# Scan stage of a two-layer network on one core: the sum over the states as turned tiles, turned back ahead of the gate

## The chip, the core and the metric

The kernel runs on one core of a Trainium2 chip. The core has TensorE (matrix products into PSUM), VectorE, ScalarE and GpSimd, each with a queue of its own, and a queue (SyncE) that issues the transfers here. The engines wait for each other by semaphores. The metric is the time of one execution on the device in microseconds (us); less is better.

## What is computed

Two layers on x of shape (2, 2048, 128). Layer 0 is a Mamba block that runs forwards and backwards over the sequence, then a mixture of experts; layer 1 is retention and another mixture of experts. The change touches the Mamba block alone:

```python
u, z = split(x @ in_w.T, 2)                 # 256 channels each
u = silu(causal_conv4(u) + conv_b)
dbc = u @ xproj_w.T                         # rank 64, B: 16 states, C: 16 states
dt = softplus(dbc[..., :64] @ dt_w.T + dt_b)
def step(h, inp):                           # for each channel d and each state n
    h = exp(dt * A) * h + dt * u * B
    return h, einsum('bdn,bn->bd', h, C)    # the sum over the 16 states
y = ys + u * D
return y * silu(z) @ out_w.T                # the gate, and the output projection
out = x + mamba(x, forwards) + mamba(reversed x, backwards)
```

## The kernel before

All of it is float32, apart from the parts of B and C that are spread over the partitions. The Mamba stage works in 16 units (`UNITS`): 8 chunks of 512 positions, each once forwards (even units) and once backwards (odd units). The 256 channels are two halves (`HF`) of 128 partitions; a tile "128x1024" is both halves of a chunk. In a unit there are 16 steps, one for each state n; `s` counts all 256 steps. The five engines run lists of their own, written out by hand; each list goes through the steps s in order and has in it, at given n, the work for the chunk after next or the next (`prep(m + 1, n)`).

For a state s the work goes like this:

- ScalarE makes the decays exp(dt * A), one half at a time, into one of four PSUM banks `pa` (`decays`, line 588). These banks are slots: `handed()` (line 269) writes out in which order things are put into them, item i goes to `pa[i % 4]`, and item i may be written once item i - 4 has been taken (`s_taken`, counted by VectorE). Per unit the squares and the relu of the next chunk's dt pass through the same slots.
- The inflow dt*u*B is made by VectorE (`inflow`, line 731, with B spread by TensorE in `spread_b`) for nine of the states, by GpSimd (line 876) for the seven in `BY_G` = 1, 3, 5, 7, 9, 13, 15.
- VectorE scans (`scan`, line 742): one instruction for each half, in place in one of six buffers `hh`.
- GpSimd multiplies with C into one of four buffers `hc` (`times_c`, line 888); before writing the buffer of state s it waits until TensorE has added state s - 4.
- TensorE adds up (`add_up`, line 409): with the identity as weights and `hc` as the 512 moving columns, into the two PSUM banks `py`. TensorE does it four steps late (`LAG` = 4). The first product of a unit is the D term: `uz` times the diagonals `dd`. It waits for the gate of the unit before (`s_gate`), since `py` is one pair of banks.

After scan 3 of the next unit (`n == LAG - 1`) VectorE does the gate (line 757): `yz` = silu(z) times `py`, one instruction of 128x1024. TensorE's output projection (`out_project`) of that unit comes at n = 8 and 9 of the next unit but one in its own list (`prep(m + 1, n)`), that is in the unit after the gate's; ScalarE collects it (`collect`, line 583). In the list of ScalarE, n = 3 has the copies of rank and high part (`rank_and_high`), n = 5 the middle part (`mid_part`, line 506); VectorE takes the rest of high at n = 4 and the low part at n = 5 (`low_part`, line 699), and TensorE waits for the low part before dt is projected (n = 6).

At the end of the last unit nothing follows in this stage: the last sum, gate, projection and collection come one after the other, and then all engines meet (`phase_end`).

GpSimd's list has per unit 16 products with C, 7 inflows and, at n = 12, dt times u of the next chunk (line 867), for which VectorE's first inflow of the next unit waits.

## Time and profile before

| | before |
|---|---|
| time, median of 3 runs | 1487.87 us (1487.68 to 1488.51) |
| the profiled execution: span from first to last instruction | 1526.0 us |
| TensorE busy, matrix products | 1319.7 us, 86% |
| VectorE busy | 1240.1 us, 81% |
| GpSimd busy | 1154.2 us, 76% |
| ScalarE busy | 968.7 us, 63% |
| mean granted clock of TensorE, share of 2.4 GHz | 0.964 |

The profile is of one execution, which takes longer than the runs that are timed. The Mamba stage is its first part, up to about 933 us. In the rows PE is TensorE's products, PEld its weight loads, DVE VectorE, ACT ScalarE, POOL GpSimd; L423 is line 423 of the kernel. A row of instructions has output<-inputs, shapes, xcount. An f32 product shows as two records. The two levels of TensorE's clock are 1.00 (2.4 GHz) and 0.50 (1.2 GHz). Who ended a wait is inferred; where the engine named had long been done it was another.

### The profile page before, as it was taken

Reading aid. Unit: us, or ns where it says so; the run is one execution under the profiler, and the core shown is the slowest. Engines: PE = TensorE matmul, PEld = TensorE weight load, DVE = VectorE, ACT = ScalarE, POOL = GpSimd, SP = SyncE. Lnnn points to the kernel's source line nnn. Section 1 sums busy time; section 2 is a strip of 40 time slices with the busy share of each in tenths; the row PEclk is TensorE's granted clock in tenths of the full one; section 3 lists DMA queues with packets and bytes.
Section 4 is the critical chain, followed back from the end, with each engine's and each line's share of the span. In section 5 each row is a group of like instructions: output and inputs, shape, how many; then the busy total and the mean of one; then the engine's idle time right before and its main releaser. Section 6 shows DMA issues by size and latency. Waiting matters only on the chain.

```text
span 1526.0 us, 19904 instructions
## 1 busy us (share of the span) xinstructions
PE 1319.7 (86%) x6159; PEld 760.5 (50%) x6159; DVE 1240.1 (81%) x1990; ACT 968.7 (63%) x1810; POOL 1154.2 (76%) x683
## 2 busy tenths in 40 slices
PE   6799889889988988988988878988998999997595
PEld 2234334334434433433433334558996666666594
DVE  6999999999999999999999996323335888876376
ACT  6887878878778777787787774214554555542144
POOL 2899999999999999999999992611333555583542
PEclk9999999999999999999999989999999999999698
DMA  5323322333343333342333224131216000011223
GB/s 194 116 86 123 133 106 104 133 119 111 122 129 113 123 105 114 122 127 93 122 133 107 99 104 188 52 82 41 80 52 220 2 1 2 2 55 32 79 68 96
DMA packets 62888, 148.38 MB, mean 97 GB/s; under 512 B 9216, under 2 KB 34304, under 8 KB 53072
## 3 DMA queue, kind: packets, MB, share of 16 engines
q1 hardware_dynamic: 58016, 137.30, 26.6%
q0 software_dynamic: 4768, 9.81, 2.0%
q8 instruction: 51, 0.84, 0.2%
q14 instruction: 53, 0.43, 0.1%
HBM read 134.14 MB, written 18.56 MB: 100 GB/s over the span
## 4 chain that ended last, share of the span: by engine, by line
PE 32%; DVE 25%; issue 15%; POOL 12%; ACT 10%; another core or an unknown queue 3%; DMA 2%; SPq 1%; DVEq 0%; POOLq 0%; ACTq 0%
DVE hh L754 15%; POOL hc L895 8%; DVE hh L739 3%; PE py L423 3%; ACT pa L598 3%; PE pr L1806 3%; PE bank L1352 2%; PE bank L1348 2%; PE bank L1362 2%; POOL dtu L874 2%; PE pr L1820 2%; PE pr L2009 2%; ACT uz L492 1%; PE bank L1268 1%
## 5 line engine op out<-in xcount | busy, mean ns | idle before, releaser
L895 POOL TENSOR_TENSOR hc<-hh,cs 128x1024 f32<-128x1024 f32 x256 | 599.3, 2369 | 3.9 <-ACT st L603 2.6
L423 PE MATMUL py<-hc,ident 128*128 128x512 f32 x1024 | 487.5, 605 | 0.1
L754 DVE TENSOR_TENSOR_SCAN hh<-pa,st,hh 128x512 f32<-128x512 f32 x384 | 466.4, 1265 | 0.5 <-ACT pa L598 0.2
L598 ACT ACTIVATE pa<-dt,w 128x512 f32<-128x512 f32 x512 | 343.8, 684 | 184.4 <-DVE hh L754 183.2
L423 PEld LDWEIGHTS py<-hc,ident 128*128 128x128 f32 x1024 | 198.3, 195 | 220.5 <-issue 211.8
L885 POOL TENSOR_TENSOR hh<-dtu,bs 128x1024 f32<-128x1024 f32 x111 | 262.4, 2365 | 2.4 <-DMA bs<-bcrows 2.4
L739 DVE TENSOR_TENSOR hh<-dtu,pb 128x1024 f32<-128x1024 f32 x145 | 174.3, 1202 | 15.1 <-POOL dtu L874 14.1
L754 DVE TENSOR_TENSOR_SCAN hh<-pa,hh 128x512 f32<-128x512 f32 x128 | 147.8, 1205 | 2.0 <-ACT pa L598 1.0
L1478 POOL DMA_INDIRECT ytoken<-ysort,token x39 | 39.6, 1016 | 112.2 <-ACT ysort L1410 111.6
L335 PE MATMUL pq<-xn,w 128*128 128x512 f32 x248 | 118.0, 600 | 4.0 <-ACT xn L613 2.8
L1851 DVE TENSOR_SCALAR rot<-pr,b 128x128 f32<-128x128 f32 x184 | 51.8, 344 | 50.0 <-PE pr L1820 21.8
L406 PE MATMUL pb<-bc,sel 96*128 96x512 bf16 x145 | 56.4, 389 | 41.6 <-DVE hh L739 41.1
L1455 DVE TENSOR_TENSOR ht<-bank,xt 128x512 f32<-128x512 f32 x39 | 27.0, 692 | 69.3 <-PE bank L1362 66.0
L1806 PE MATMUL pr<-rot 128*128 128x128 f32 x368 | 53.9, 294 | 31.5 <-ACT rot L1833 22.2
L1869 POOL DMA_INDIRECT ytoken<-rot,token x46 | 44.8, 974 | 46.4 <-DVE rot L1858 38.4
L335 PEld LDWEIGHTS pq<-xn,w 128*128 128x128 f32 x248 | 47.4, 192 | 63.6 <-issue 61.7
L419 PE MATMUL py<-uz,dd 128*128 128x512 f32 x64 | 41.7, 787 | 38.0 <-DVE yz L762 36.3
L2486 POOL TENSOR_TENSOR qr<-ra,rb 128x256 f32<-128x256 f32 x16 | 11.6, 726 | 75.8 <-DVE rb L2252 75.8
L1806 PEld LDWEIGHTS pr<-rot 128*128 128x128 f32 x368 | 48.5, 206 | 34.7 <-ACT rot L1839 18.0
L1197 POOL DMA_INDIRECT xsorted<-xn,pos x32 | 30.9, 965 | 43.2 <-DVE pos L1170 29.2
L1290 ACT ACTIVATE xt<-bank 128x512 f32<-128x512 f32 (+1 forms) x32 | 18.1, 570 | 69.5 <-PE bank L1259 54.9
L406 PEld LDWEIGHTS pb<-bc,sel 96*128 96x128 bf16 x145 | 14.1, 97 | 95.4 <-DVE hh L739 65.3
(333 smaller groups left out, 2523.6 us busy)
## 6 DMA issues: line engine op xcount, KB each, us to landing
cs<-bcrows SPq DMA_DIRECT2D x64, 1024.0 KB, 4.6
bs<-bcrows SPq DMA_DIRECT2D x112, 256.0 KB, 4.4
xsorted<-in_pads SPq DMA_DIRECT2D x13, 387.0 KB, 5.3
rot<-in_rot SPq DMA_DIRECT2D x4, 1024.0 KB, 5.0
wx<-in_l_w SPq DMA_DIRECT2D x4, 1024.0 KB, 10.0
ysort<-ytoken SPq DMA_DIRECT2D x14, 256.0 KB
wx<-in_l_w SPq DMA_DIRECT2D x1, 3072.0 KB, 11.2
wx<-in_l_w SPq DMA_DIRECT2D x1, 2304.0 KB, 16.2
```

Source lines behind the costliest of these rows:

```text
L335: i = pe.matmul(bnk[:, :], w[:, W_U + t * DI + h * P:W_U + t * DI + (h + 1) * P], tokens(m, t), start=t == 0, stop=t == TAPS - 1)
L406: pe.matmul(pb[:, :], sel[0:96, s % NS:s % NS + 1].broadcast_to([96, P]), bc[s // NS % 2][0:96, :], start=True, stop=True).then_inc(s_b, 1)
L419: pe.matmul(py[:, h * CH:(h + 1) * CH], dd[s // NS % 2][:, h, :], uz[s // NS % 2][:, h, :], start=True, stop=False)
L423: i = pe.matmul(py[:, h * CH:(h + 1) * CH], ident[:, :], hc[s % HCS][:, h, :], start=False, stop=n == NS - 1)
L598: act.activation(pa[i % SLOTS][:, :], dt[m % 2][:, h, :], ACT.Exp, scale=wd[m % 2][:, W_A + h * NS + n:W_A + h * NS + n + 1]).then_inc(s_s ...
L739: v.tensor_tensor(hh[s % HHS][:, :, :], dtu[m % 2][:, :, :], pb[:, :].unsqueeze(1).broadcast_to([P, HF, CH]), ALU.mult).then_inc(s_db, 1)
L754: v.tensor_tensor_scan(hh[s % HHS][:, h, :], pa[i % SLOTS][:, :], hh[s % HHS][:, h, :], 0.0 if first else st[:, m % 2, n, h:h + 1], ALU.mu ...
L885: g.tensor_tensor(hh[s % HHS][:, :, :], dtu[m % 2][:, :, :], bs[i // BG][:, i % BG, :].unsqueeze(1).broadcast_to([P, HF, CH]), ALU.mult).t ...
L895: g.tensor_tensor(hc[s % HCS][:, :, :], hh[s % HHS][:, :, :], cs[j % 2][:, s % CG, :].unsqueeze(1).broadcast_to([P, HF, CH]), ALU.mult).th ...
L1806: i = pe.matmul(pu[j % 2][:, f * P:(f + 1) * P], wr[j % 2][:, f * P:(f + 1) * P], xts[j % 2][:, :], start=True, stop=True)
L1851: i = v.tensor_scalar(ht[j % 2][:, f * P:(f + 1) * P], pu[j % 2][:, f * P:(f + 1) * P], b1[:, ds(e * FK + f, 1)], 0.0, ALU.add, ALU.max)
L1869: g.indirect_dma_start(out=ytoken, out_offset=bass.IndirectOffsetOnAxis(ap=token[:, j:j + 1], axis=0), in_=ysort[:, j, :], in_offset=None) ...
```

## The change

In the sum over the states data and identity change sides. Each 128x128 piece of `hc` is now the stationary operand, the identity moves (128 columns), and the product is done as a transpose (`is_transpose=True`) that adds to what is in PSUM. So `py` holds the sum with positions on the partitions: eight pieces for each state. The D term is made in the same turned form (pieces of `uz` stationary, diagonals moving). When a unit is complete, ScalarE copies both banks of `py` into a new SBUF tile `yt` (`keep_sum`, at n = 4 of the next unit, behind the decays of state 5). TensorE turns the eight pieces back (`turn_back`, at n = 4 in its list) into two of the four decay slots, which `handed()` now lists behind the decays of state 5. The gate reads these two slots, as two instructions of 128x512, and has moved from behind scan 3 to behind scan 5. The D term of the next unit waits for the copy, not for the gate; the output projection waits for the second slot to be taken. Since TensorE fills some slots, the waits for ScalarE's fillings count with `slot_count`. Not shown in the diff: the new semaphores, and one semaphore (`s_wset`) in the place of two for the start's exponentials and diagonals, with its counts.

```diff
@@ -235,6 +236,7 @@
                 yz = sb(k, "yz", [P, HF, CH])
+                yt = sb(k, "yt", [P, HF * CH])
                 hh = [sb(k, f"hh{i}", [P, HF, CH]) for i in range(HHS)]
...
@@ -271,13 +273,20 @@
                         order += [("decay", s, h) for h in range(HF)]
+                        if m >= 1 and n == LAG + 1:
+                            order += [("y", m - 1, h) for h in range(HF)]
                         if m + 1 < UNITS and n in (10, 11):
                             order += [("square", m + 1, n - 10, h) for h in range(HF)]
                         if m + 1 < UNITS and n == 12:
                             order += [("relu", m + 1, h) for h in range(HF)]
-                    return order
+                    return order + [("y", UNITS - 1, h) for h in range(HF)]

                 turn = {item: i for i, item in enumerate(handed())}
+                by_tensor = [item[0] == "y" for item in handed()]
+
+                def slot_count(i):
+
+                    return i + 1 - sum(by_tensor[:i + 1])

...
@@ -365,7 +374,7 @@
                         if of[0] == 0:
-                            pe.wait_ge(s_gate, m + 1)
+                            pe.wait_ge(s_taken, turn["y", m, HF - 1] + 1)
                             if m + 2 < UNITS:
...
@@ -408,20 +417,31 @@
                         n = s % NS
+                        tiles = [(h, kt, slice(kt * P, (kt + 1) * P)) for h in range(HF) for kt in range(4)]
                         if n == 0:
                             if s >= NS:
-                                pe.wait_ge(s_gate, s // NS)
+                                pe.wait_ge(s_yt, s // NS)
                             else:
                                 pe.wait_ge(s_xt, 6)
                             if s // NS < 2:
-                                pe.wait_ge(s_diag, (HF + 1, 2 * HF + 1)[s // NS])
-                            for h in range(HF):
-                                pe.matmul(py[:, h * CH:(h + 1) * CH], dd[s // NS % 2][:, h, :], uz[s // NS % 2][:, h, :],
-                                          start=True, stop=False)
+                                pe.wait_ge(s_wset, (HF + 2, 2 * HF + 3)[s // NS])
+                            for h, kt, t in tiles:
+                                pe.matmul(py[:, h * CH + kt * P:h * CH + (kt + 1) * P], uz[s // NS % 2][:, h, t], dd[s // NS % 2][:, h, :],
+                                          start=kt == 0, stop=False)
                         pe.wait_ge(s_hc, s + 1)
+                        for h, kt, t in tiles:
+                            i = pe.matmul(py[:, h * CH + kt * P:h * CH + (kt + 1) * P], hc[s % HCS][:, h, t], ident[:, :],
+                                          is_transpose=True, start=False, stop=n == NS - 1 and kt == 3)
+                        i.then_inc(s_ysum, 1)
+
+                    def turn_back(m):
+                        pe.wait_ge(s_yt, m + 1)
                         for h in range(HF):
-                            i = pe.matmul(py[:, h * CH:(h + 1) * CH], ident[:, :], hc[s % HCS][:, h, :], start=False, stop=n == NS - 1)
-                        i.then_inc(s_ysum, 1)
+                            i = turn["y", m, h]
+                            pe.wait_ge(s_taken, i - SLOTS + 1)
+                            for kt in range(4):
+                                mm = pe.transpose(pa[i % SLOTS][:, kt * P:(kt + 1) * P], yt[:, h * CH + kt * P:h * CH + (kt + 1) * P], ident[:, :])
+                            mm.then_inc(s_yback, 1)

...
@@ -466,9 +486,12 @@
                             add_up(s - LAG)
+                        if n == LAG and m >= 1:
+                            turn_back(m - 1)
                         prep(m + 1, n)
                     for s in range(STEPS - LAG, STEPS):
                         add_up(s)
+                    turn_back(UNITS - 1)
                     out_project(UNITS - 1, (0, 1))
...
@@ -598,6 +621,13 @@

+                    def keep_sum(m):
+
+                        act.wait_ge(s_ysum, NS * (m + 1))
+                        if m >= 1:
+                            act.wait_ge(s_yback, HF * m)
+                        act.activation(yt[:, :], py[:, :], ACT.Identity).then_inc(s_yt, 1)
+
                     def keep_state(s):
...
@@ -670,6 +700,8 @@
                             diagonals(1)
+                        if s % NS == LAG and s >= NS:
+                            keep_sum(s // NS - 1)
                         prep(s // NS + 1, s % NS)
...
@@ -688,6 +720,7 @@
                     scalar_normed(xn, range(NT - 4, NT))
+                    keep_sum(UNITS - 1)
                     collect(UNITS - 1)
...
@@ -704,7 +737,7 @@
                             i = turn["square", m, f, h]
-                            v.wait_ge(s_slot, i + 1)
+                            v.wait_ge(s_slot, slot_count(i))
                             if f > 0:
...
@@ -750,17 +783,18 @@
                             i = turn["decay", s, h]
-                            v.wait_ge(s_slot, i + 1)
+                            v.wait_ge(s_slot, slot_count(i))
                             v.tensor_tensor_scan(hh[s % HHS][:, h, :], pa[i % SLOTS][:, :], hh[s % HHS][:, h, :],
                                                  0.0 if first else st[:, m % 2, n, h:h + 1], ALU.mult, ALU.add).then_inc(s_taken, 1)

                     def gate(m):
-                        v.wait_ge(s_ysum, NS * (m + 1))
                         if m >= 1:
                             v.wait_ge(s_op, m)
                         v.wait_ge(s_uz, m + 2)
-                        v.tensor_tensor(yz[:, :, :] if m % 2 == 0 else yz[:, :, ::-1], uz[(m + 1) % 2][:, HF:2 * HF, :],
-                                        view(py, HF, CH), ALU.mult).then_inc(s_gate, 1)
+                        for h in range(HF):
+                            v.wait_ge(s_yback, HF * m + h + 1)
+                            v.tensor_tensor(yz[:, h, :] if m % 2 == 0 else yz[:, h, ::-1], uz[(m + 1) % 2][:, HF + h, :],
+                                            pa[turn["y", m, h] % SLOTS][:, :], ALU.mult).then_inc(s_taken, 1)

...
@@ -855,7 +889,7 @@
                             vector_moments(range(t.start, t.stop))
-                        if n == LAG - 1 and m >= 1:
+                        if n == LAG + 1 and m >= 1:
                             gate(m - 1)
```

## Rows read from the trace of the kernel before

**Rows 1.** Window of the scan stage: stretch, its us, busy (count) per engine, clock, DMA.

```profile
core 0: us, PE busy (x) PEld busy (x) DVE busy (x) ACT busy (x) POOL busy (x), PEclk, DMA share, GB/s
100.00:926.00 826.00, 720.57 (x1891) 316.38 (x1889) 806.03 (x803) 634.90 (x1110) 826.00 (x358) 0.97 0.34 115
```

**Rows 2.** Waits: engine and line waited for releaser: us in total, times, longest.

```profile
POOL hc L895 <- ACT st L603: 2.6, 1, 2.6
POOL hc L895 <- DVE hh L754: 1.2, 1, 1.2
DVE hh L739 <- POOL dtu L874: 14.1, 9, 2.7
```

**Rows 3.** Groups up to 960 us: busy us, mean ns of one, idle before.

```profile
L423 PE MATMUL py<-hc,ident 128*128 128x512 f32 x1024 | 487.5, 605 | 0.1
L379 PE MATMUL pq<-w,yz 128*128 128x128 f32 x256 | 39.0, 275 | 0.0
L710 DVE SCALAR_TENSOR_TENSOR dt<-pa,dt 128x512 f32<-128x512 f32 x32 | 20.2, 674 | 0.0
L530 ACT ACTIVATE ww<-ab 128x1024 f32<-128x1024 f32 x16 | 16.7, 1046 | 0.0
L1074 PE MATMUL bank<-ident,xn 128*128 128x128 f32 x32 | 4.1, 276 | 0.7 <-ACTq L106 0.7
```

**Rows 4.** Timeline of TensorE, merged: start, us, what, count, [idle before <-releaser].

```profile
537.00 3.60 PE L423 MATMUL py<-hc,ident 128*128 128x512 f32 x8
...
933.28 2.40 PE L1074 MATMUL bank<-ident,xn 128*128 128x128 f32 x20 [0.72 <-ACTq L106]
```

**Rows 5.** Timelines of ScalarE, TensorE and GpSimd in unit 6.

```profile
385.87 0.19 ACT L603 ACTIVATE st<-hh 128x2 f32<-128x2 f32 x1
386.56 0.69 ACT L598 ACTIVATE pa<-dt,w 128x512 f32<-128x512 f32 x1 [0.51 <-DVE hh L754]
...
388.58 0.59 ACT L508 ACTIVATE bc<-pq 32x512 bf16<-32x512 f32 x1
...
385.39 3.64 PE L419 MATMUL py<-uz,dd 128*128 128x512 f32 x4 [2.43 <-DVE yz L762]
...
394.27 4.69 POOL L895 TENSOR_TENSOR hc<-hh,cs 128x1024 f32<-128x1024 f32 x2
```

**Rows 6.** Short windows, columns as in rows 1; the last but two is the clock.

```profile
71.60:74.90 3.30, 3.30 (x6) 1.01 (x5) 3.30 (x4) 3.27 (x5) 0.98 (x1) 0.50 0.67 278
382.20:385.40 3.20, 0.77 (x4) 0.06 (x2) 3.20 (x4) 3.16 (x8) 3.20 (x3) 1.00 0.71 243
385.60:388.90 3.30, 3.30 (x5) 1.24 (x5) 3.24 (x4) 2.29 (x6) 3.30 (x2) 0.50 0.03 5
388.90:392.30 3.40, 3.40 (x9) 1.44 (x8) 3.37 (x4) 1.17 (x3) 3.40 (x3) 0.99 0.00 0
932.40:937.10 4.70, 2.56 (x22) 2.17 (x20) 3.14 (x13) 3.66 (x9) 0.00 (x0) 1.00 0.42 86
```

**Rows 7.** Timelines of TensorE, VectorE and GpSimd in unit 0, states 9 to 11.

```profile
71.47 3.54 PE L423 MATMUL py<-hc,ident 128*128 128x512 f32 x4
...
71.10 2.32 DVE L754 TENSOR_TENSOR_SCAN hh<-pa,hh 128x512 f32<-128x512 f32 x2
...
79.02 2.32 DVE L754 TENSOR_TENSOR_SCAN hh<-pa,hh 128x512 f32<-128x512 f32 x2
...
75.15 2.36 POOL L895 TENSOR_TENSOR hc<-hh,cs 128x1024 f32<-128x1024 f32 x1 [2.57 <-ACT st L603]
...
79.78 4.69 POOL L895 TENSOR_TENSOR hc<-hh,cs 128x1024 f32<-128x1024 f32 x2
```

**Rows 8.** Timeline of the last unit's end, from 926 us.

```profile
923.89 2.37 POOL L895 TENSOR_TENSOR hc<-hh,cs 128x1024 f32<-128x1024 f32 x1
925.75 2.55 PE L423 MATMUL py<-hc,ident 128*128 128x512 f32 x5
...
928.34 1.22 DVE L762 TENSOR_TENSOR yz<-uz,py 128x1024 f32<-128x1024 f32 x1 [2.91 <-PE py L423]
...
929.61 0.49 PE L376 MATMUL pq<-residual,ident 128*128 128x128 f32 x2 [1.31 <-DVE yz L762]
```

17 lines of the change are left out of this document (9 added, 8 removed).

## Prediction

> **What bounds the kernel now.** I read three views, from the wide to the narrow. The window from 100 to 926 us comes first; it is nearly fifteen of the scan stage's sixteen units. In it GpSimd is busy for all 826.00 us, VectorE for 806, TensorE for 721 and ScalarE for 635 [rows 1]. Three engines over four fifths say nothing yet about who sets the end; a row without a hole does. GpSimd runs 358 instructions in those 826 us, 2.307 us each. A unit has 24 of them (16 products with C, 7 inflows, one dt times u), so it takes 55.4 us whatever the others do. The waits say it from the other side: VectorE waited 14.1 us for GpSimd's dt times u, in nine units, while GpSimd's products with C lost 1.2 us once to a scan and 2.6 us once to something else [rows 2]; both are ahead of 100 us, in unit 0. The timelines show who ends which wait at the places below. So GpSimd is the pace. TensorE, whose work the change rewrites, follows with room: it can matter only where a product with C needs the buffer that TensorE must have read (four products back), at that hole of 2.6 us, and in the last unit's end, where nothing follows.
>
> **The change part by part.**
>
> *Adding a state up.* Before, a state's sum is two products of 512 columns, four records. Eight records in a row take 3.60 us [rows 4], one alone 0.6 [rows 3], so (3.60 - 0.6) / 7 = 0.43 each, 1.72 us a state and 0.16 of drain. After, it is eight turned tiles of 128x128. The trace has turned tiles of this size and type: twenty in a row take 2.40 us [rows 4], one 0.28 [rows 3], so 2.12 / 19 = 0.112 us each. What it doesn't show is turned tiles that add to what stands in PSUM. From below I bound that by the same 0.112 us, from above by the ordinary 128x128 f32 product: it has two records, each as long as a turned tile's, 275 against 276 ns [rows 3], so 0.224 us a tile. That makes 0.90 to 1.79 us a state against 1.72. I take 0.90, since the nearest row is the same operation but for a flag. Over a unit TensorE is relieved of 16 x 0.82 = 13.1 us (or given 1.1).
>
> *The D term.* It was four records of 0.43 us; now it is 16 records of 128 columns at 0.112 us: 1.8 against 1.72. Nothing. The renamed counters and the bookkeeping of slots have one answer: nothing.
>
> *The copy by ScalarE.* 128x1024 out of PSUM. ScalarE's squares of that size take 1.05 us [rows 3]. Fifteen of the sixteen lie beside other work: ScalarE is free for a quarter of the stretch [rows 1]. In its order the copy stands behind the decays of state 5. I follow unit 6. There ScalarE has done those decays and the small state copy at 385.87 + 0.19 = 386.06 and then waits 0.5 us for VectorE [rows 5]. The new copy takes 386.06 to 387.1. Queued behind it are the decays of state 6.
>
> *Turning back.* Eight transposes, 0.90 us of TensorE a unit. TensorE used to wait for the gate until 385.39, 2.4 us of it idle [rows 5]; now it waits for the copy until 387.1. Behind that wait stand the D term and the sums of states 0 and 1. State 0 is in at 387.1 + 0.9 + 1.8 + 0.9 + 0.2 = 390.9. GpSimd's product of state 4, which needs that buffer, starts at 394.27 [rows 5]: slack 3.4 us. If the clock falls in the longer idle time and stays down for the whole chain, it is 387.1 + 2 x 3.6 + 0.2 = 394.5, 0.2 us late. (Unit 6's D term did run at 1.2 GHz, 3.64 us [rows 5, 6], and the clock was back right behind it [rows 6].) I put 0 and keep 0.2 x 15 = 3 us as the bound.
>
> *Two decay slots for the gate, and the gate two states later.* The gate leaves its place behind scan 3 and comes behind scan 5. Scans 4 and 5 move 1.1 us forward, the rest keeps its place. As two instructions of 128x512 it costs 2 x 0.67 less 0.08 of overlap, 1.26 us (VectorE's dt products out of PSUM [rows 3]), against 1.22 [rows 8]: nothing to speak of. But ScalarE's decays of state 6 now wait for scan 5 instead of scan 4, since the gate sits in the other two slots. Their second half ends some 0.7 us behind scan 5; behind it stand the state copy and the middle part of B and C (0.59 us, at 388.58 before [rows 5]), for which VectorE's low part waits: 1.4 us behind scan 5 in all. The gate covers 1.26 of that; with the hop from engine to engine a stall of 0.2 to 0.3 us is left. VectorE has it: at the end of nine units it still waits for GpSimd [rows 2], and in all of the fifteen no instruction of GpSimd had to wait [rows 1]. So nothing at the end; without that cover it would be 0.3 x 15 = 4.5 us.
>
> *A hole closes in unit 0.* TensorE's sum of state 5 starts at 71.47 and takes 3.54 us, at 1.2 GHz [rows 6, 7]. GpSimd is free at 75.15 - 2.57 = 72.58 and starts its product of state 9 at 75.15. The row names ScalarE's state copy as the releaser; but what ended 0.14 us before is that sum, which the product waits for too. The sum will take 1.06 us (2.0 at 1.2 GHz). Late next is scan 9, which ends at 73.42: GpSimd gains 75.15 - 73.5 = 1.65 us. But its product of state 11 started at 79.78 + 2.31 = 82.09, and scan 11 ends at 81.34 [rows 7]: VectorE has no hole there and comes no earlier, so 0.75 us of the gain is left. I take -0.75, bounds -1.65 and 0.
>
> *The last unit.* What is added here is on the path. Before: GpSimd's last product is ready at 926.26, the sum at 928.30, the gate starts at 928.34, the output projection at 929.61 [rows 8]. After, from 926.3: eight tiles 1.06 -> 927.4; copy 1.05 -> 928.5; turning back, first half 0.6 -> 929.15, second 1.05 -> 929.6; gate halves to 929.8 and 930.5; projection 930.55. That is +0.94 us. With those sixteen tiles at 1.2 GHz it is +2.2. I take +0.9.
>
> Sum on the profiled execution's own time: 1526.0 - 0.75 + 0.9 = 1526.2 us. That execution is 38 us longer than the median of the runs, 1487.87; I carry the difference over one to one: 1488.0 us.
>
> **The rivals.**
>
> *A: the clock stays down.* TensorE's work a unit goes from 721 / 826 x 55.4 = 48.3 us to 48.3 - 13.1 + 0.9 = 36.1, 65% busy. What precedes a fall the trace shows: from 382.2 to 385.4 TensorE was busy 0.77 of 3.2 us, and behind that the clock stood at 0.50, 1.2 GHz [rows 6]. If turned tiles didn't count as activity, the ten light states of each unit would run at 1.2 GHz. The six others hold 5.4 us of sums, twenty projection records of 0.43 and three spreads of 0.2, 14.6 in all; the light ones 21.5, which becomes 43.0 where 10/16 of 55.4 = 34.6 are to be had: +8.4 us a unit, +125 in all, 1613 us. Against it: from 932.4 to 937.1 TensorE did little but twenty turned tiles, 2.56 of 4.7 us, and kept 1.00 [rows 6]. Chance 0.05.
>
> The Trainium skill (TensorE: Matmul & The Clock Gate, Part 4: PE-mode transpose) states just this, that full clock doesn't engage for transposes, which don't count as busy in the same way. By that rule the change would make the kernel slower by this rival's sum; the one stretch of this trace that bears on it disagrees.
>
> *B: the turned sum comes late to GpSimd.* Slower, at state 4 of every unit from the second on. Copy, turning back, D term and first sum are one chain of 8.2 us at half clock, and it decides from the point where state 0 is added later than GpSimd's 394.27. With the copy 0.5 us late (a scan holds ScalarE) and half clock throughout it is 0.7 us a unit, +10 us: 1498. For it: TensorE will idle some 4 us ahead of the chain. Against: 3.4 us of slack at full clock, and in unit 6 a busy TensorE had its clock back within 3.4 us. Chance 0.09.
>
> *C: GpSimd gets quicker.* If its 2.307 us hold some contention with TensorE's reading, which the change alters, 0.4% of it would be -4 us: 1484. Against: its pace holds in unit 6 and over the fifteen units, whatever TensorE's clock and work. Chance 0.06.
>
> *D: the change doesn't relieve TensorE* (an adding turned tile costs 0.224 us). TensorE is then as busy as before, the hole in unit 0 shrinks little, and the end is 1 to 2 us above the forecast, inside its range.
>
> **How the numbers follow.** The forecast with D has 0.80: 1488.0, from 1487.0 to 1490.5 (hole -1.65 to 0, end +0.9 to +2.2, some scatter). A measurement of this kernel can't tell less than about 0.2%, 3 us, from no change. So same 0.80, faster 0.06 (C), slower 0.14 (A, B). The range takes in the forecast's own and reaches towards C and B: 1485.5 to 1491.5.
>
> **What would show it.** Right: GpSimd without a hole from 100 us on; TensorE's busy time down by some 200 us at the same span; the projection of the last unit about 4.3 us behind GpSimd's last product instead of 3.35; the hole ahead of GpSimd's product of state 9 in unit 0 near 0.9 us; more falls of the clock. Wrong: idle time of GpSimd put down to TensorE's sums (B), a granted clock near 0.7 in the scan stage (A), GpSimd's instructions under 2.3 us a piece (C), or VectorE so late behind the gate that it no longer waits for dt times u and GpSimd waits for scans.

## The result and the profile after

The changed kernel takes 1493.48 us (median, 1491.29 to 1494.53), the kernel before 1487.87: the ratio is 1.0039, with a 95% interval from 1.0022 to 1.0056, so some 5.6 us slower. The forecast was 1488.0 with a range up to 1491.5, so the time lies 2.0 us above the range. The direction was to be "the same", and it is slower, by little but clear of the interval.

One warning ahead of the reading. The profiled execution of before (span 1526.0 us) comes from a chip on which everything *behind* the scan stage takes 592.9 us; the one of after (span 1489.3) from a chip where it takes 552.6. The instructions there are the same. That the chip makes the difference is inferred from the experiments, where the kernel before takes 1525.7 us on one chip and 1487.0 on another. So the 38 us by which the profile of before exceeds its timed runs are not what profiling costs; since the forecast carried them over one to one, they changed nothing in it. The two spans say nothing about the change, and I compare the scan stage alone, up to the end of its last instruction, ScalarE's last collecting copy: 933.19 us before, 936.73 after.

The page of after, its first lines, in the columns of the page of before:

```profile
span 1489.3 us, 22655 instructions
PE 1192.3 (80%) x7503; PEld 878.4 (59%) x7503; DVE 1237.8 (83%) x2006; ACT 981.3 (66%) x1826; POOL 1155.3 (78%) x683
```

TensorE has 127 us less to do, GpSimd and VectorE what they had. The window that answers to [rows 1], and GpSimd's and VectorE's waits up to 937 us, which answer to [rows 2]:

```profile
100.00:926.00 826.00, 608.91 (x3155) 431.38 (x3154) 803.39 (x816) 644.78 (x1126) 824.73 (x356) 0.87 0.33 114
```

```profile
POOL hc L929 <- DVE hh L787: 0.8, 1, 0.8
POOL hc L929 <- PE py L433: 0.2, 1, 0.2
...
DVE hh L772 <- POOL dtu L908: 12.5, 9, 2.7
...
DVE bc L735 <- ACT bc L531: 4.5, 14, 0.3
```

GpSimd (the missing 1.27 us are the stretch behind its last instruction) still sets the pace without a hole. Its instructions come a little less often: from the first product with C of unit 1 to the last one of unit 15 there are 355 steps, (923.89 - 102.92) / 355 = 2.3126 us before, (922.33 - 99.92) / 355 = 2.3166 after. The granted clock is down from 0.97 to 0.87.

The end, which answers to [rows 8]. First windows around it, after:

```profile
912.40:917.80 5.40, 4.78 (x25) 4.35 (x25) 5.40 (x9) 1.86 (x5) 5.40 (x4) 0.66 0.01 2
917.80:922.90 5.10, 2.61 (x20) 2.14 (x21) 3.79 (x8) 1.46 (x3) 5.10 (x4) 1.00 0.02 3
922.90:936.70 13.80, 10.60 (x47) 9.10 (x44) 1.78 (x5) 3.74 (x8) 1.82 (x1) 0.51 0.00 0
```

The same of before:

```profile
917.80:922.90 5.10, 5.10 (x13) 2.28 (x12) 5.10 (x9) 0.20 (x1) 5.10 (x3) 0.98 0.00 0
922.90:933.20 10.30, 8.34 (x37) 4.61 (x35) 1.86 (x5) 4.00 (x8) 3.36 (x2) 1.00 0.00 1
```

And the timeline of after, from the last sum to the last collecting copy:

```profile
924.78 1.97 PE L433 MATMUL py<-ident,hc 128*128 128x128 f32 x8 [0.70 <-POOL hc L929]
926.78 1.02 ACT L629 ACTIVATE yt<-py 128x1024 f32<-128x1024 f32 x1 [1.21 <-PE py L433]
...
927.86 1.97 PE L443 MATMUL pa<-ident,yt 128*128 128x128 f32 x8 [1.11 <-ACT yt L629]
929.11 1.44 DVE L796 TENSOR_TENSOR yz<-uz,pa 128x512 f32<-128x512 f32 x2 [5.22 <-PE pa L443]
...
930.61 0.79 PE L385 MATMUL pq<-residual,ident 128*128 128x128 f32 x2 [0.78 <-DVE yz L796]
...
935.03 1.06 PE L388 MATMUL pq<-w,yz 128*128 128x128 f32 x4
936.13 0.60 ACT L609 ACTIVATE residual<-pq 128x512 f32<-128x512 f32 x1 [8.32 <-PE pq L388]
```

TensorE stood at 2.4 GHz while it was busy 2.61 of 5.10 us, and then at 1.2 GHz for all of the end: the last sum and the turning back 1.97 us each, and the output projection from 930.61 to 936.1, 5.5 us, where before it took 3.0. The projection starts 5.88 us behind the end of GpSimd's last product, before it was 3.35 us. So of the 5.09 us that the end is longer, 2.5 lie ahead of the projection and 2.5 in it.

Where the stage's time went, by the starts of GpSimd's products with C. "Start" is the first of unit 0, "unit 0" from there to the first of unit 1, "units 1 to 15" from there to the very last, "end" from there to the end of the last collecting copy (before and after: 9.30 and 14.39 us). Each line is the second kernel less the first, in us, out of one profile each; the lower lines are experiments, below.

| pair | start | unit 0 | units 1 to 15 | end | sum |
|---|---|---|---|---|---|
| before, after (full) | -0.20 | -2.80 | +1.44 | +5.09 | +3.54 |
| e0_before, e0_after (full) | +0.99 | -1.92 | +1.05 | +2.67 | +2.79 |
| sc_before, sc_after (stage alone) | -0.14 | +0.04 | +1.05 | +2.60 | +3.57 |
| sc_before_neg, sc_after_neg | +0.13 | +1.12 | +0.88 | +3.40 | +5.53 |
| sc_before_neg, sc_last_old_neg | +0.18 | -0.18 | +0.92 | -0.08 | +0.83 |

Two columns repeat in their sign, the end and units 1 to 15. Unit 0 doesn't, and that has to be explained before its -2.80 is counted as a gain.

The size of the end's column varies, and one reason lies in the kernel before. Its end takes 9.3 to 9.45 us in three profiles (before, sc_neg, sc_before_neg) and 10.2 to 10.3 in two (e0_before, sc_before). The stretch ahead differs in the clock, here before and then sc_before:

```profile
914.60:918.10 3.50, 3.50 (x6) 1.42 (x5) 3.50 (x8) 2.03 (x5) 3.50 (x3) 0.51 0.00 0
```

```profile
910.90:917.70 6.80, 5.61 (x8) 2.43 (x9) 6.80 (x11) 3.87 (x9) 6.80 (x4) 0.50 0.00 0
```

TensorE has no hole from there to the last sum. With 6.8 us at 1.2 GHz in place of 3.5 it falls behind with the thick sums and ends the last one 2.9 us behind GpSimd's last product, not 2.0. So 0.9 of the 5.09 us is that the profile of before has the short end.

### The profile page after: what moved, and what is told of

It is laid out like the page before. It is cut to its first block, busy times and chain, and to the rows that moved or that the text cites. A ratio compares the mean times of both kernels' runs of the same rounds, so it can differ in the third digit from the quotient of the medians.

```text
span 1489.3 us, 22655 instructions
## 1 busy us (share of the span) xinstructions
PE 1192.3 (80%) x7503; PEld 878.4 (59%) x7503; DVE 1237.8 (83%) x2006; ACT 981.3 (66%) x1826; POOL 1155.3 (78%) x683
## 4 chain that ended last, share of the span: by engine, by line
PE 35%; DVE 18%; POOL 15%; issue 15%; ACT 14%; DMA 2%; SPq 0%; DVEq 0%; POOLq 0%; ACTq 0%
DVE hh L787 11%; POOL hc L929 10%; ACT pa L621 5%; POOL hh L919 3%; DVE hh L772 2%; PE bank L1386 2%; PE bank L1396 2%; PE bank L1382 2%; POOL dtu L908 2%; PE pr L1840 2%; PE pr L2043 2%; PE py L433 2%; PE bank L1302 2%; ACT uz L515 2%; PE pr L1854 2%
## 5 line engine op out<-in xcount | busy, mean ns | idle before, releaser
L433 PEld LDWEIGHTS py<-ident,hc 128*128 128x128 f32 x2048 | 263.8, 153 | 80.0 <-issue 58.0
L433 PE MATMUL py<-ident,hc 128*128 128x128 f32 x2048 | 290.7, 293 | 5.2 <-POOL hc L929 5.2
L919 POOL TENSOR_TENSOR hh<-dtu,bs 128x1024 f32<-128x1024 f32 x111 | 266.5, 2402 | 3.0 <-DMA bs<-bcrows 3.0
L772 DVE TENSOR_TENSOR hh<-dtu,pb 128x1024 f32<-128x1024 f32 x145 | 174.3, 1202 | 13.0 <-POOL dtu L908 12.5
L344 PE MATMUL pq<-xn,w 128*128 128x512 f32 x248 | 121.2, 614 | 26.8 <-ACT pre L507 22.5
L415 PE MATMUL pb<-bc,sel 96*128 96x512 bf16 x145 | 59.7, 412 | 79.6 <-DVE hh L772 79.6
L344 PEld LDWEIGHTS pq<-xn,w 128*128 128x128 f32 x248 | 43.9, 196 | 63.5 <-issue 37.9
L360 PE MATMUL pq<-uz,w 128*128 128x512 f32 x64 | 59.3, 1081 | 21.0 <-ACT uz L515 21.0
L354 PE MATMUL pq<-xn,w 128*128 128x512 f32 x60 | 41.6, 782 | 37.8 <-ACT pre L507 37.4
L443 PE MATMUL pa<-ident,yt 128*128 128x128 f32 x128 | 27.2, 382 | 42.0 <-ACT yt L629 42.0
L1840 PE MATMUL pr<-rot 128*128 128x128 f32 x368 | 50.1, 280 | 10.5 <-DVE rot L1885 7.6
```

Of the source, the lines that this page charges most:

```text
L344: i = pe.matmul(bnk[:, :], w[:, W_U + t * DI + h * P:W_U + t * DI + (h + 1) * P], tokens(m, t), start=t == 0, stop=t == TAPS - 1)
L360: i = pe.matmul(pq[:, :], wd[m % 2][:, W_X + h * P:W_X + (h + 1) * P], uz[m % 2][:, h, :], start=h == 0, stop=h == HF - 1)
L415: pe.matmul(pb[:, :], sel[0:96, s % NS:s % NS + 1].broadcast_to([96, P]), bc[s // NS % 2][0:96, :], start=True, stop=True).then_inc(s_b, 1)
L433: i = pe.matmul(py[:, h * CH + kt * P:h * CH + (kt + 1) * P], hc[s % HCS][:, h, t], ident[:, :], is_transpose=True, start=False, stop=n == ...
L772: v.tensor_tensor(hh[s % HHS][:, :, :], dtu[m % 2][:, :, :], pb[:, :].unsqueeze(1).broadcast_to([P, HF, CH]), ALU.mult).then_inc(s_db, 1)
L919: g.tensor_tensor(hh[s % HHS][:, :, :], dtu[m % 2][:, :, :], bs[i // BG][:, i % BG, :].unsqueeze(1).broadcast_to([P, HF, CH]), ALU.mult).t ...
```

## The experiments

**First set: full kernels.** e0_before and e0_after are the two kernels once more on one chip. e1_last_old is the changed kernel with its last unit done the old way (abridged: its D term and its gate are in the old form too):

```diff
+ if s // NS == UNITS - 1:      # D term and sums of the last unit
+     for h in range(HF):
+         i = pe.matmul(py[:, h * CH:(h + 1) * CH], ident[:, :], hc[s % HCS][:, h, :], start=False, stop=n == NS - 1)
- turn_back(UNITS - 1)
- keep_sum(UNITS - 1)
```

> The kernel before, unchanged, profiled and timed again beside itself. It settles three readings of the first two profiles. (1) The profile of before has a span of 1526.0 us, 38 us over its timed median, the one of after 1489.3 us: if that is a disturbance behind the scan stage, the new profile has a span of about 1486 us with the scan stage ending at 933 us again. (2) GpSimd's spacing in the scan stage was 2.3125 us a piece in before and 2.3165 in after. If that is the change (pace theory), this run shows 2.3125 again, within 0.5 ns; if it is scatter from execution to execution (scatter theory), it comes out anywhere from 2.311 to 2.317. (3) VectorE's second negation (128x32) took 2.01 us in before and 0.38 in after: if that is a matter of where it falls in GpSimd's instruction, it is 2.0 here again.

> The changed kernel, unchanged, once more. Ratio to before 1.003 to 1.005. Cold-end theory: from GpSimd's last product to the end of the collection it takes 13 to 14.4 us where before takes 9.3, with a granted clock near 0.5 there, and the timed runs scatter by 3 us because the clock's falls lie elsewhere each time. Pace theory: spacing 2.3165 again. Scatter theory: spacing the same as in the repeated kernel before.

> The change undone in the last unit alone: its sixteen sums, its D term and its gate are those of before (512 moving columns, gate straight from the sum's banks, no copy, no turning back); units 0 to 14 are as in the changed kernel. Cold-end theory: the end, from GpSimd's last product to the collection's end, is 9.3 us again, clock near 1, and the kernel is 4 to 5 us faster than the changed one: 1488.5 us, the same as before or up to 1 us faster (unit 0's hole is smaller). Pace theory as the whole cause: the end's length doesn't matter, and it stays at 1492 to 1493.

e2_warm_end is the changed kernel with idle products in the last unit's end (not shown: ahead of the last four sums TensorE waits until VectorE has made its last inflow, since the idle products overwrite the spread B):

```diff
+ def keep_warm(times):
+     for _ in range(times):
+         pe.matmul(pb[:, :], sel[0:96, 0:1].broadcast_to([96, P]), bc[(UNITS - 1) % 2][0:96, :], start=True, stop=True)
  for s in range(STEPS - LAG, STEPS):
      add_up(s)
+     keep_warm(4)
  turn_back(UNITS - 1)
+ keep_warm(4)
```

> The changed kernel with twenty idle products added in TensorE (128x512 bf16, results not used, 0.22 us each): four behind each of the last four sums and four behind the turning back, where TensorE waits anyway. They lengthen no chain and only keep TensorE busy. If the clock is what the end costs, the granted clock stays at 1.0 there, the end takes 10.3 us (9.3 plus the 0.94 of the forecast's own chain) and the kernel is 3.5 to 4 us faster than the changed one: 1489.5. If the chain itself (copy, turning back, two gates) is what costs, nothing moves: 14.4 us of end and 1493.

Measured (kernel before on this chip: 1525.9 us):

| run | us | ratio to before | end, us | clock in it | behind the stage, us |
|---|---|---|---|---|---|
| e0_before | 1525.7 | 0.9996 [0.9985, 1.0007] | 10.26 | 1.00 | 594.3 |
| e0_after | 1523.1 | 0.9984 [0.9969, 1.0000] | 12.93 | 0.74 | 585.7 |
| e1_last_old | 1526.8 | 1.0006 [0.9993, 1.0020] | 9.84 | 1.00 | 587.9 |
| e2_warm_end | 1520.5 | 0.9974 [0.9960, 0.9988] | 10.56 | 1.00 | 582.1 |

The end is short again where the last unit is the old one or the clock is held, and the times don't follow: on this chip the part behind the stage differs by 12 us between kernels that are the same there, and hides the stage. Each of these parts is from one profile, and some of the 12 us is scatter: the profile of e0_before is of its slowest execution (1528.8 us), that of e1_last_old of its fastest (1522.2). With the stage's end of each profile taken off the median, some 7 us are left between the kernels (an estimate). So the times of this set decide nothing about the stage. They missed what I expected: e0_after was to be 1.003 to 1.005 of before, e1_last_old 4 to 5 us faster than the changed kernel and was 3.7 slower, e2_warm_end 3.5 to 4 us faster and was 2.6, and e0_before's span was to be about 1486 us and was 1526.9.

A difference sits some 40 to 75 us behind the barrier, in the shared expert, where the trace names no releaser that it knows. VectorE's waits from 935 to 1060 us in e0_before, and in e0_after (second fence):

```profile
DVE ht L1304 <- remote: 15.1, 2, 7.7
```

```profile
DVE ht L1338 <- remote: 6.1, 1, 6.1
```

In the profile of after, from the quicker chip, no such row stands in that stretch. Its cause I did not find.

**Second set: the scan stage alone.** All four leave out everything behind the stage's barrier and store the residual as it stands:

```diff
  layer0_mamba()
+ for tile in range(0, NT, 8):
+     sy.dma_start(out[:, tile:tile + 8, :], bx[:, tile:tile + 8, :]).then_inc(s_out, 16)
+ sy.wait_ge(s_out, NT // 8 * 16)
+ return
```

sc_last_old and sc_warm add the edits of e1 and e2.

> The scan stage of the kernel before alone: everything behind the stage's barrier is left out, and the residual is stored as the stage leaves it. It measures nothing of the two theories by itself; it is the foot that the three others of this set are compared with, without the 550 to 590 us behind the stage, whose length differed by up to 12 us between kernels that are the same there. Expected: end of the last collecting instruction at 932 to 934 us of the span (933.2 and 932.7 in the two full runs), GpSimd's spacing 2.313 us, an end of 9.3 to 10.3 us behind the last product with C, and a time of some 950 us (an estimate: 933 plus the barrier and one store of the residual).

> The scan stage of the changed kernel alone, with nothing behind its barrier. Theory 1 (the whole loss is at the end of the stage, made of the clock that has fallen by then, and a little in the spacing of GpSimd's instructions, with a gain in unit 0): slower than the stage before by 2.5 to 4 us, as +3.5 and +2.8 us at the barrier in the two full pairs, so a ratio of 1.003 to 1.004; the end 13 to 14.5 us behind the last product with C with the granted clock under 0.75 there. Theory 2 (the loss of the full kernel lies behind the stage, in what the changed one leaves to the code that follows): within 1 us of the stage before.

> The scan stage alone, the changed kernel but for its last unit, which is summed and gated in the old way (thick sums, no copy, no turning back, one gate on the sum). Theory 1: the end shrinks to 9.3 to 10 us, the gain in unit 0 (2 to 3 us) stays, and GpSimd's spacing costs 1 to 1.4 us back, so 0.5 to 2 us faster than the stage before. Rival (the losses sit in the fourteen units between, not at the end): still 2 us or more slower than the stage before.

> The scan stage alone, the changed kernel with twenty idle 128x512 products on TensorE in the last unit, behind the last four sums and behind the turning back, into a bank that nobody reads any more. It leaves nothing out and adds no step to the chain except what lies in front of it on TensorE. Theory 1 with the clock as the larger part of the end: clock near 1.0 there, the end 10.3 to 11.3 us, and the stage within 1 us of the stage before, 2 to 3.5 us below the changed stage without them. Rival (the three new steps themselves are the larger part, the clock is not): no more than 1 us below the changed stage.

| run | median, us | five runs | end, us | clock in it |
|---|---|---|---|---|
| sc_before | 940.32 | 940.17 to 941.20 | 10.24 | 1.00 |
| sc_after | 944.98 | 943.40 to 945.48 | 12.84 | 0.73 |
| sc_last_old | 942.23 | 940.14 to 942.40 | 9.84 | 1.00 |
| sc_warm | 942.48 | 940.93 to 943.07 | 10.57 | 1.00 |

The stage itself loses 4.7 us, so the loss is in it; I had expected 2.5 to 4. The chip is one on which the full kernel before takes 1525.4 us, about as in the first set, where the full kernels didn't show the loss; the changed full kernel was not run on this one. The old last unit takes 2.8 us of that back, the idle products 2.5. The end of sc_warm, with the same three steps as in after:

```profile
926.41 1.09 PE L433 MATMUL py<-ident,hc 128*128 128x128 f32 x8 [0.47 <-POOL hc L936]
...
927.82 1.00 ACT L636 ACTIVATE yt<-py 128x1024 f32<-128x1024 f32 x1
...
928.88 1.09 PE L447 MATMUL pa<-ident,yt 128*128 128x128 f32 x8 [0.51 <-ACT yt L636]
929.67 1.28 DVE L803 TENSOR_TENSOR yz<-uz,pa 128x512 f32<-128x512 f32 x2 [3.44 <-PE pa L447]
...
931.01 0.49 PE L385 MATMUL pq<-residual,ident 128*128 128x128 f32 x2 [0.17 <-DVE yz L803]
```

Sum and turning back take 1.09 us, and the end is only 0.33 us longer than sc_before's. In sc_after the clock fell later than in after, at about 927.2, behind the last sum, and rose at about 934.0, ahead of the projection's last quarter:

```profile
919.00:925.30 6.30, 2.65 (x22) 1.95 (x20) 4.22 (x11) 2.12 (x5) 6.24 (x3) 1.00 0.01 3
...
927.70:934.10 6.40, 5.57 (x25) 5.17 (x26) 1.37 (x2) 0.00 (x0) 0.00 (x0) 0.51 0.00 0
934.10:936.00 1.90, 0.99 (x9) 0.80 (x8) 0.00 (x0) 0.60 (x1) 0.00 (x0) 1.00 0.00 0
```

That is the difference between an end of 12.84 and one of 14.39. My expectation missed for sc_last_old (0.5 to 2 us faster than before; it was 1.9 slower), since the gain in unit 0 that I counted on was not there, and for sc_warm (within 1 us; 2.2 slower): against sc_before its profile has 0.3 us in the end, 1.2 in units 1 to 15, and a unit 0 of 59.79 us, 1.15 longer.

**Third set: unit 0, the spacing, and a shorter end.** In unit 0 one small VectorE instruction, the second sign change of the decay rates, differed between profiles. sc_before's VectorE and GpSimd there, and then after's:

```profile
61.15 2.03 DVE L800 TENSOR_SCALAR w<-w 128x32 f32<-128x32 f32 x1
63.10 1.21 DVE L739 TENSOR_TENSOR hh<-dtu,pb 128x1024 f32<-128x1024 f32 x1
...
60.78 2.36 POOL L885 TENSOR_TENSOR hh<-dtu,bs 128x1024 f32<-128x1024 f32 x1
63.09 2.38 POOL L895 TENSOR_TENSOR hc<-hh,cs 128x1024 f32<-128x1024 f32 x1
```

```profile
61.71 0.38 DVE L834 TENSOR_SCALAR w<-w 128x32 f32<-128x32 f32 x1
62.01 1.21 DVE L772 TENSOR_TENSOR hh<-dtu,pb 128x1024 f32<-128x1024 f32 x1
...
62.01 2.37 POOL L919 TENSOR_TENSOR hh<-dtu,bs 128x1024 f32<-128x1024 f32 x1
```

Both times it ends where GpSimd starts its next instruction. In sc_before it started 0.4 us behind the start of one of GpSimd's and took 2.03 us; in after 0.3 us ahead of the next one, and took 0.38. sc_neg takes it away from VectorE:

```diff
  decay_rates(1)
+ act.wait_ge(s_wexp, 2)
+ act.activation(wd[1][:, W_A:W_N], wd[1][:, W_A:W_N], ACT.Identity, scale=-1.0).then_inc(s_wneg, 1)
- negated(1)
```

> The scan stage before the change, alone, with one edit that has nothing to do with it: the second sign change of the decay rates (128x32) is made by ScalarE behind its exponential, not by VectorE. Theory: in unit 0 that instruction holds VectorE for 1.9 to 2.2 us wherever it starts early in one of GpSimd's instructions, and 0.4 us where it happens to start near the end of one, and this coincidence, not the sum, made unit 0 2.8 us shorter in the changed kernel's profile. Then unit 0 takes 56.6 to 57.2 us here in place of 58.6, and the stage is 1.5 to 2 us faster than the stage before. Rival (the sum's rows held unit 0): 58.6 us and no gain.

Unit 0 took 56.92 us in place of 58.64, as expected. The time was 937.78 us (936.65 to 940.06), 2.5 us less than sc_before's where I expected 1.5 to 2, but on another chip, and with the short end of the kernel before (9.29 us) where sc_before had the long one. ScalarE does the sign change in 0.23 us. So most of the -2.80 was this coincidence: the sign change was quick in the profiles of after, e0_after and e1_last_old, slow in those of sc_after, sc_last_old, sc_warm and e2_warm_end, and slow in all three of the kernel before.

The other 0.7 us is the hole that the prediction named, and it was so large in one of three profiles of the kernel before. GpSimd's holes ahead of its products of states 9 and 11 are 2.57 and none in before, but 0.93 and 0.92 in e0_before and 1.63 and 0.22 in sc_before; in sc_after and e2_warm_end, with the sign change slow as well, they are 1.12 and 0.71. That is 1.85 us in two of three profiles of the kernel before and 1.83 after the change.

sc_thick is sc_after with thick sums (and the D term in the old form), sc_busy is sc_after with TensorE kept busy by zeros (both abridged):

```diff
- i = pe.matmul(py[:, h * CH + kt * P:h * CH + (kt + 1) * P], hc[s % HCS][:, h, t], ident[:, :], is_transpose=True, ...)
+ i = pe.matmul(py[:, h * CH:(h + 1) * CH], ident[:, :], hc[s % HCS][:, h, :], start=False, stop=n == NS - 1)
- mm = pe.transpose(pa[i % SLOTS][:, kt * P:(kt + 1) * P], yt[:, ...], ident[:, :])
+ pe.matmul(pa[i % SLOTS][:, :], ident[:, :], yt[:, h * CH:(h + 1) * CH], start=True, stop=True).then_inc(s_yback, 1)
```

```diff
+ for _ in range(4):
+     pe.matmul(py[:, 0:CH], zero[:, 0:P], zero[:, :], start=False, stop=False)
  pe.wait_ge(s_hc, s + 1)
```

> The changed scan stage alone, with the sums made the old way: D term and states go into the sum untransposed, as 128x512 products with the identity, and one more such product for each half takes the place of turning back. The copy by ScalarE, the two decay slots, the gate in halves two states later and the longer end stay. Theory 1 (the clock that the thin sums let fall is the larger part of the end, and the thin sums are what spaces GpSimd's instructions by 3 ns more): clock near 0.97 and 1.0 in the end; the copy 1.0 us, the two products on the copy 1.7 us (two of the 16 or so that go into 3.6 us in unit 6), two gates 1.4 us in place of one of 1.2, so an end of 12.5 to 13.5 us (an estimate: 10.24 + 1.0 + 1.7 + 0.2 and the hand-overs); spacing back at 2.312 to 2.313 us. Rival (the copy, the slots and the later gate space them): spacing stays at 2.315 us.

> The changed scan stage alone, with four idle 128x512 products on TensorE in each state, zeros added into the sum ahead of the wait for the state's product with C; nothing is left out. It holds TensorE's busy time where it was before the change and leaves the thin sums as they are. Theory 1: clock 0.97 or more, the end 10.3 to 11.3 us as in the kernel with idle products in the last unit alone. If GpSimd's wider spacing is the clock's doing (TensorE's reads stretched), it falls back to 2.313 us; if it is the thin sums' own (their loads of the stationary side, their number), it stays at 2.315 us or goes up.

sc_thick took 966.15 us (964.74 to 966.47). Its end was shorter than I had reckoned (12.5 to 13.5), 11.96 us at clock 1.00, but what decides is in the middle, GpSimd's wait for the sums:

```profile
POOL hc L926 <- PE py L433: 24.3, 14, 2.7
```

With thick sums, the copy, the turning back and the D term behind it are too long a chain for GpSimd's state 4: twelve of those 14 waits are at state 4 of units 2 to 15, the other two in unit 0. The relief by the turned pieces, worth nothing by itself, is what pays for the detour. The steps between GpSimd's instructions that have no wait in them were 2.3131 us on average, against 2.3126 in sc_before and 2.3156 in sc_after, at a granted clock of 0.94 from 100 to 920 us; so the copy, the slots and the later gate don't widen them, the turned pieces do.

sc_busy took 951.08 us (949.34 to 952.64), a miss: GpSimd waited 6.3 us for sums in eight places, the end was 13.01 us, not 10.3 to 11.3, and the clock over the stage was 0.95, not 0.97. TensorE's timeline there:

```profile
932.59 1.04 PE L438 MATMUL py<-ident,hc 128*128 128x128 f32 x8
933.46 1.03 PE L435 MATMUL py<-zero 128*128 128x512 bf16 x4
934.33 1.04 PE L438 MATMUL py<-ident,hc 128*128 128x128 f32 x8
936.48 1.09 PE L448 MATMUL pa<-ident,yt 128*128 128x128 f32 x8 [1.11 <-ACT yt L634]
```

The zeros ran ahead of the sums without a pause, and the last sum began 2.8 us behind the end of GpSimd's last product (931.5): I had put the idle work on the chain. What it does show: eight turned pieces take 933.46 - 932.59 = 0.87 us when TensorE runs on, and with the clock at 0.95 the steps of GpSimd that have no wait in them were 2.3171 us, not narrower. The wider spacing is not the low clock's doing.

sc_best shortens the old end, on top of sc_neg's edit. The last sum is released by halves and the last gate is two instructions (not shown), and TensorE's order changes (abridged):

```diff
+ for kt in range(4):                      # residual: ahead of the gate
+     pe.matmul(pq[:, kt * P:(kt + 1) * P], ident2[:, :], bx[:, ...], start=kt == 0, stop=False)
+ for h in range(HF):                      # a half's projection beside the other half's gate
+     pe.wait_ge(s_gate, UNITS + h)
+     for kt in range(4):
+         i = pe.matmul(pq[:, kt * P:(kt + 1) * P], yz[:, h, ...], wd[1][:, ...], start=False, ...)
```

> The stage before the change, alone, with the sign change on ScalarE, and an end made shorter in the other direction: the last state's sum is released by halves, the last gate runs in two halves, the four products that add the residual go ahead of it, and the first half's projection goes while the second half is gated. Expected: end 7.5 to 8.5 us in place of 10.24 (an estimate: 0.6 from the gate's first half beside the sum's second, 1.3 to 2 from the eight of twelve products that go ahead of the last gate), and with the shorter unit 0 3 to 4.5 us faster than the stage before. If the end is not set by this chain, no more than sc_neg gives.

936.92 us (935.46 to 937.49), its end 7.94 us, as reckoned. Against sc_neg the time gained 0.9 us where the end gained 1.35: in its profile unit 0 took 58.04 us, 1.1 more than sc_neg's, though the two kernels are the same there.

**Fourth set: the same question without the coincidence.** sc_neg's edit in the stage before, in the changed stage, and in the one with the old last unit; and the full kernel before with the edits of sc_best (e3_best, nothing left out).

> The scan stage before the change, alone, with the second sign change on ScalarE: the same kernel as sc_neg, once more so that it stands on the chip of the two below. Expected as there: unit 0 in 56.6 to 57.2 us, end 9.3 or 10.3 us, time 937 to 939 us.

> The changed scan stage alone, with the second sign change on ScalarE, so that the coincidence in unit 0 can favour neither side. Theory 1: against the stage before with the same edit, the change gives nothing in unit 0 (within 0.3 us), costs 1.0 to 1.4 us in GpSimd's spacing (2.315 in place of 2.3125 us) and 2.6 to 5 us in the end (12.8 to 14.4 us), so 3.5 to 6 us in all. Rival (the shorter unit 0 was the change's own gain): the gain stays, and the sum is 2 us or less.

> The same, with the last unit summed and gated in the old way. Theory 1: the end is that of the stage before, and only the spacing is left, so 0.7 to 1.8 us slower than the stage before with the same edit. Rival (units 1 to 14 lose more than the spacing shows, or nothing): 2.5 us or more, or within 0.4 us.

> The full kernel before the change, with the sign change on ScalarE and the shortened end (sum released by halves, gate in halves, residual products ahead, first half projected beside the second gate). Nothing is left out. From the stage alone (3.4 us less than the stage before, between chips): 2 to 4 us faster than the kernel before, a ratio of 0.997 to 0.9987, and 7 to 9 us faster than the changed one. If what follows the stage gives the gain back, within 1 us of the kernel before.

| run | median, us | runs | unit 0 | step of GpSimd | end |
|---|---|---|---|---|---|
| sc_before_neg | 937.57 | 937.00 to 938.95 | 56.97 | 2.3127 | 9.45 |
| sc_after_neg | 942.75 | 942.53 to 944.75 | 58.09 | 2.3151 | 12.85 |
| sc_last_old_neg | 939.34 | 937.92 to 941.05 | 56.79 | 2.3152 | 9.37 |
| e3_best | 1481.66 | 1480.81 to 1484.83 | 57.02 | 2.3129 | 7.69 |

The change costs the stage 5.2 us. With the last unit done in the old way 1.8 us are left, of which the spacing explains 0.9; so the end is the larger part, 3.4 us. sc_after_neg's unit 0 was 1.1 us longer, not within 0.3 as expected: its profile has two waits for scans at 44.6 and 59.1 us (0.42 and 0.48 us) that sc_before_neg's doesn't have, and sc_last_old_neg's neither. Such waits occur without the change too: GpSimd in sc_best, whose unit 0 is that of sc_before_neg, waits 0.43 us at 45.5 us and 0.80 at 57.9, and its unit 0 is as long (58.04). What puts them there in some executions stays open.

e3_best is faster than the kernel before, which took 1487.01 us on its chip: ratio 0.9970, from 0.9958 to 0.9981, 5.3 us by the medians where I expected 2 to 4. Behind the stage its profile takes 550.4 us, that of after 552.6, with the same instructions there; whether some of the full kernel's 5.6 us lies in this part isn't shown. Its end:

```profile
923.68 1.45 PE L436 MATMUL py<-hc,ident 128*128 128x512 f32 x3
...
924.38 1.48 DVE L778 TENSOR_TENSOR yz<-uz,py 128x512 f32<-128x512 f32 x2 [2.08 <-PE py L436]
...
924.96 1.05 PE L369 MATMUL pq<-residual,ident 128*128 128x128 f32 x8
...
925.86 1.95 PE L374 MATMUL pq<-w,yz 128*128 128x128 f32 x16
927.84 0.60 ACT L600 ACTIVATE residual<-pq 128x512 f32<-128x512 f32 x1 [3.86 <-PE pq L374]
```

## Why the prediction was wrong, step by step

**What bounds the kernel**: right. GpSimd has no hole from 100 us to its last product, VectorE still waits for its dt times u in nine units (12.5 us, 14.1 in [rows 2]). The 2.307 us a piece were slightly low, since the 358 instructions of the window include cut ones; from start to start it is 2.3126.

**Adding a state up**, 0.90 us: right. At 2.4 GHz the eight pieces take 0.87 us where TensorE runs on (sc_busy's timeline). TensorE's busy time was to fall by some 200 us; it fell by 127. The sums alone gave 487.5 - 290.7 = 197 [rows 3]. The rest went back: 27.2 us of turning back, and other products that now meet the low clock, the projection to B, C and dt above all, 663 ns a record before and 1081 after.

**Copy, turning back, the two slots**: right in size and in that nothing of it reaches the end. The copy took 1.00 us. The low part's wait for ScalarE is there as reckoned, 0.3 us, 14 times, and is covered. The slack at state 4 was thinner than the 3.4 us I followed. Unit 6 after the change:

```profile
384.49 1.76 PE L443 MATMUL pa<-ident,yt 128*128 128x128 f32 x7 [3.10 <-ACT yt L629]
386.25 3.62 PE L429 MATMUL py<-dd,uz 128*128 128x128 f32 x16
389.67 2.28 PE L433 MATMUL py<-ident,hc 128*128 128x128 f32 x16
...
391.77 4.74 POOL L929 TENSOR_TENSOR hc<-hh,cs 128x1024 f32<-128x1024 f32 x2
```

State 0 is in at about 390.8 (half of 2.28 us behind 389.67), GpSimd's state 4 begins at 391.77: 1.0 us is left, since turning back and D term ran at 1.2 GHz (0.50 granted from 384.7 to 389.8). My bound for that case, 0.2 us late, was the right one to carry.

**A hole closes in unit 0**, -0.75: right for the execution that was read, and not a gain of the change. That profile of before had holes of 2.57 us where the other two had 1.85 and the changed kernel 1.83. Unit 0 as a whole was 0.04 us longer in one pair of stages alone and 1.1 in the other, and 1.1 us more occurs without the change too (sc_best). The -2.80 of the full profiles would have looked like a better gain than forecast; 2 us of it was the sign change. In the kernel before, that instruction was in plain sight and I didn't read it.

**The last unit**, +0.94, and +2.2 "with those sixteen tiles at 1.2 GHz": this is the step that failed. Its structure was right: with the clock held up the end is 10.56 and 10.57 us, 1.1 to 1.3 longer than the short ends of the kernel before (9.30 to 9.45) and 0.3 longer than the long ones (10.24 and 10.26); I had said 0.94, from a short one. The other 0.3 us is ScalarE, which has the normalising of four tiles (1.65 us) ahead of the copy in its list and starts it 0.3 us behind the last sum; I had put that wait at nothing.

What the step left out is that the change itself takes the clock away there. The sums of the last four states had held TensorE at 5.10 busy of 5.10 us; after, it is 2.61 of 5.10, and the clock falls. And it priced the low clock for the sixteen tiles alone, while the 24 records of the projection behind them, which the change doesn't touch, pay as well: 5.5 us in place of 3.0.

The +2.2 was small for the sixteen tiles too: sum and turning back are 0.9 us longer each at 1.2 GHz, less the 0.2 us that the second half of the gate had to spare, which with the 0.94 makes 2.6 us; +2.5 was measured ahead of the projection. In all, sum, turning back and projection gave +5.1 where the clock was down throughout, and +2.6 to +3.4 where it was down for 6.8 us of the end (+3.4 against a short end of the kernel before, +2.6 and +2.7 against the long ones).

**What was in no step**: the turned pieces widen GpSimd's step by 2.5 to 4 ns, +0.9 to +1.4 us over 355 steps. I had only the other direction, as rival C. Why they do is open; that it is the pieces and neither the copy nor the clock is what sc_thick and sc_busy show. Another 0.9 us of sc_last_old_neg's 1.8 us is unexplained and within the scatter of its runs.

**The rivals.** A had the right resource and the wrong place: the clock did fall to 0.87 on average, but TensorE had the room for it in fifteen units, and only in the end it had none. Its strong form, that turned tiles count for nothing, isn't borne out: from 912.4 to 917.8 us TensorE of after did one spread of 0.6 us and turned pieces, and the clock came up in it (0.66 over the window, 1.00 behind it). The Trainium skill (TensorE: Matmul & The Clock Gate, Part 4: PE-mode transpose) says that transposes don't count as busy in the same way; that stretch disagrees, as the one that the prediction quoted. B did not occur with turned pieces, and occurred with thick ones, 24.3 us. D is refuted: TensorE is relieved.

## What to carry to other kernels

When a change makes an engine idle, follow its clock to the place where the engine is next on the path, and price everything that it does there at the low clock, the old work too. Relief of an engine that isn't the bound can cost time in this way; work that nobody needs, put behind the sums of the last states, made the end 2.3 us shorter (12.84 to 10.57). And before a difference in a profile is counted for a change, look for a second profile: an instruction of 0.4 us that took 2 us in some executions was as large as a good part of what was being measured.

## What the runs showed of the hardware

- VectorE's 128x32 sign change in unit 0 ended where GpSimd's running instruction ended, in all twelve profiles that have it on VectorE: 0.38 to 0.57 us in three that began it near that end, 1.39 us in sc_thick, which began it 1.0 us behind GpSimd's start, 1.8 to 2.2 us in the other eight. The larger ones beside it (128x1024 at 1.21 us, scans at 1.2) don't wait in this way. Moved to ScalarE it took 0.23 us, and unit 0 got 1.7 us shorter (58.64 to 56.92).
- Eight turned f32 tiles that add into PSUM: 0.87 us in a row at 2.4 GHz, 1.97 alone with the drain at 1.2.
- TensorE at 2.61 busy of 5.10 us, all turned tiles: the clock held there and was at 1.2 GHz right behind, for 13.8 us. In sc_after it held 2.65 of 6.30 us and fell later. I don't know what decides between the two.
- The clock's fall ahead of the end costs the kernel before as well: its end is 10.2 to 10.3 us with 6.8 us at 1.2 GHz ahead of it (e0_before, sc_before), 9.3 to 9.45 with 3.5 us (before, sc_neg, sc_before_neg).
- The same instructions behind the scan stage take 550 to 553 us in two profiles and 582 to 594 in five, and the timed full kernel before 1487.0 us on one chip and 1525.7 on another.
